# Scores for the maximum in four quarters through one PSUM bank of their own, and six PSUM banks for the layers after the last exp

## What is computed

```python
s = jnp.einsum('bqhd,bkhd->bhqk', q, k) * scale
s = jnp.where(mask, s, jnp.finfo(s.dtype).min)   # only in the first block
a = jax.nn.softmax(s, axis=-1)
return jnp.einsum('bhqk,bkhd->bqhd', a, v)
...
h = jax.nn.gelu(xm @ mlp_W1 + mlp_b1, approximate=True)
h = jax.nn.silu(jnp.einsum('btc,ecr->bter', combined, e_w1) + e_b1)
g = jax.nn.sigmoid(jax.nn.silu(combined @ gate_w1 + gate_b1) @ gate_w2 + gate_b2)
```

## Time and profile before

| | |
|---|---|
| median of 3 runs | 800.41 us (796.43 to 803.18) |
| profiled execution | 800.15 us, span 798.3 us |
| PE busy | 648.6 us (81%) |
| PE weight loads busy | 364.3 us (46%) |
| DVE busy | 431.4 us (54%) |
| ACT busy | 419.8 us (53%) |
| POOL busy | 220.0 us (28%) |
| mean granted TensorE clock | 0.944 |

### The profile page before, as it was taken

The page is one execution under the profiler, slowest core; times in us unless marked ns, Lnnn a source line. Parts: engine busy times, 40 slices in busy tenths (PEclk is TensorE's granted clock), DMA queues, the critical chain, the costliest instruction groups (busy, mean ns, idle before and its releaser), DMA issues.

```text
span 798.3 us, 16559 instructions
## 1 busy us (share of the span) xinstructions
PE 648.6 (81%) x6694; PEld 364.3 (46%) x6732; DVE 431.4 (54%) x1121; ACT 419.8 (53%) x714; POOL 220.0 (28%) x319
## 2 busy tenths in 40 slices
PE   5579887888879987888788878888899788868887
PEld 5234443444444544445345444543456443644445
DVE  2447767646665676566655666666555652231222
ACT  0141634555465464736474457365676639465453
POOL 3142433305341434323431334143131420000000
PEclk9689999998989999999999899999999989989899
DMA  8500000000000000000000000000000000000000
GB/s 302 175 2 1 16 1 15 14 2 28 15 1 2 15 14 15 2 14 15 16 1 2 24 5 2 15 1 15 1 2 14 2 1 2 0 14 1 0 14 13
DMA packets 15314, 15.81 MB, mean 20 GB/s; under 512 B 1833, under 2 KB 13108, under 8 KB 14856
## 3 DMA queue, kind: packets, MB, share of 16 engines
q1 hardware_dynamic: 14572, 10.72, 4.5%
q10 hardware_dynamic: 668, 4.05, 1.3%
HBM read 13.66 MB, written 1.09 MB: 18 GB/s over the span
## 4 chain that ended last, share of the span: by engine, by line
PE 51%; ACT 27%; DVE 15%; issue 4%; POOL 1%; DMA 1%; SPq 0%; DVEq 0%; ACTq 0%; POOLq 0%
ACT P L576 13%; PE lin L938 12%; PE lin L951 9%; PE big L1027 8%; PE avp L1055 6%; DVE mhl L773 5%; PE big L1006 3%; ACT hT L559 3%; ACT xn L548 2%; PE big L1034 2%; DVE bst L725 2%; PE big L1022 2%; ACT hid L610 2%; PE lin L960 2%; DVE oT L805 1%
## 5 line engine op out<-in xcount | busy, mean ns | idle before, releaser
L773 DVE TENSOR_REDUCE mhl<-big 128x8 bf16<-128x616 f32 (+1 forms) x160 | 151.0, 963 | 95.0 <-PE big L1006 92.6
L504 POOL TENSOR_TENSOR qm<-qT,hm 128x512 f32<-128x512 f32 x80 | 88.0, 1100 | 125.8 <-ACT qT L541 77.3
L938 PE MATMUL lin<-hT,W 128*128 128x512 f32 x184 | 107.7, 673 | 14.5 <-ACT hid L610 6.1
L576 ACT ACTIVATE P<-big,padcol 128x1024 f32<-128x1024 f32 x64 | 67.9, 1114 | 73.0 <-PE big L1034 73.0
L576 ACT ACTIVATE P<-big 128x1024 f32<-128x1024 f32 x64 | 62.0, 1021 | 78.0 <-PE big L1034 77.9
L1027 PE MATMUL big<-qm,kT 32*128 32x512 f32 x640 | 99.7, 695 | 0.0
L467 POOL TENSOR_SCALAR rstd<-mv 128x4 f32<-128x4 f32 (+1 forms) x36 | 8.4, 233 | 313.7 <-DVE mv L731 313.5
L1055 PE MATMUL avp<-P,Vp 128*32 128x128 f32 x2560 | 91.0, 285 | 1.3 <-DVE Vp L740 1.2
L490 POOL TENSOR_TENSOR kbm<-kT,hm 128x308 bf16<-128x308 f32 (+1 forms) x80 | 68.2, 853 | 58.0 <-PE big L1006 47.9
L1055 PEld LDWEIGHTS avp<-P,Vp 128*32 128x32 f32 x2560 | 68.2, 113 | 29.0 <-issue 24.5
L1006 PE MATMUL big<-kbm,qb 32*128 32x308 bf16 (+1 forms) x320 | 54.6, 342 | 29.0 <-ACT P L576 27.5
(11 more groups left out here) (160 smaller groups left out, 929.7 us busy)
## 6 DMA issues: line engine op xcount, KB each, us to landing
gring<-gate_rows SPq DMA_DIRECT2D x20, 256.0 KB, 3.5
W<-in_w ACTq DMA_DIRECT2D x2, 1152.0 KB, 12.3
hid<-in_ws SPq DMA_DIRECT2D x2, 832.0 KB, 5.5
W<-in_w ACTq DMA_DIRECT2D x1, 1088.0 KB, 7.3
x<-in_x SPq DMA_DIRECT2D x4, 256.0 KB, 9.9
out<-x SPq DMA_DIRECT2D x4, 256.0 KB, 2.0
ctx<-in_ctx SPq DMA_DIRECT2D x4, 154.0 KB
ctxT<-in_ctxT SPq DMA_DIRECT2D x4, 154.0 KB
```

Of the source, the lines that this page charges most:

```text
L504: nc.gpsimd.tensor_tensor(qm[:, j % 2], q.broadcast_to([128, 4, T]), mask.broadcast_to([128, 4, T]), ALU.mult).then_inc(qm_ready, 1)
L576: nc.scalar.activation(P[:, 8 * half:8 * half + 8, :], big[:, 2 * half:2 * half + 2, :].rearrange("p g (h q) -> p (g h) q", h=4), ACT.Exp, ...
L773: v.tensor_reduce(mhl[:].rearrange("p (g c) -> p g c", c=32)[:, 2 * half:2 * half + 2, 0:4], big[:, 2 * half:2 * half + 2, 0:4 * kw].rearr ...
L938: i = mm(lin_ap(st, s, job, m)[:, 0:n], w, a, start=(c == 0), stop=(c == len(parts) - 1))
```

## The change

- The scores for the maximum get a bank of their own, `sc`, of one bank (`GQ` = 1). They come in four quarters (`NQ` = 4) of one group of heads, and a quarter of job u + 1 stands in each slot of job u. A quarter is written when the maximum of the quarter before it has been read from `sc` (a wait for `m_ready`).
- `big` holds only transposed scores. `scores_t(u)` waits for both exps of job u - 1 (`st_free`), and the subtraction is a function of its own, `subtract(u)`, in slot 1. The exps move to slot 1 with it.
- `av(u - 1)` moves from slot 3 to the start of slot 0 of the next job, ahead of `turn(u)`.
- `normalise` is cut in two: two instructions in slot 0 behind the first quarter's maximum, two in slot 1 (`normalised`).
- `keep_warm` and its bank go; the transposed maxima go to a free part of the bank `avp`.
- Behind `END`, the layer units go round six banks (two of `lin`, four of `big`).
- The chains of layer units start two slots later and end two slots earlier.

```diff
@@
+NQ = 4
+GQ = 4 // NQ
+NLIN = 2
...
-TAILS = [(16 * 14, 16 * 18), (16 * 17, END + 16), (16 * 19, END + 60), (END + 16, END + 76)]
+TAILS = [(16 * 14 + 2, 16 * 18), (16 * 17 + 2, END + 16), (16 * 19 + 2, END + 60), (END + 16, END + 76)]
...
-    end = 16 * POS[k, s] - 6
+    end = 16 * POS[k, s] - 8
     if k:
-        return 16 * (POS[k - 1, s] + 1), end
+        return 16 * (POS[k - 1, s] + 1) + 2, end
...
+    if _kind == "END":
+        _ended, _next = True, 0
...
+            _bank = _next % (NLIN + 4 if _ended else NLIN)
+            _uses[_bank] += 1
+            LIN_AT[(_u[0], _s, _job)] = _bank, _uses[_bank]
...
-        mtpf = ps("mtp", [128, 512])
-        mtp = mtpf[:].bitcast(BF16)
+        sc = ps("sc", [128, GQ, 512])
+        mtp = avp[:].bitcast(BF16)[:, 4 * T:5 * T]
...
-                elif kind == "A" and s == 0:
+                elif kind == "A" and s == 1:
                     exps(u, 0)
                     exps(u, 1)
...
-            def maxima(j, half):
+            def maxima(j, part):
 
                 kw = ATT[job_of(j)[0]]["kw"]
-                dve.wait_ge(s_full, job_turn(j, half, 2))
+                dve.wait_ge(s_full, job_turn(j, part, NQ))
...
                     if s == 0:
                         turned(u)
-                        if u > 0:
-                            normalise(u - 1)
-                    elif s < 3 and u + 1 < JOBS:
-                        maxima(u + 1, s - 1)
+                    if u + 1 < JOBS and s % GQ == 0:
+                        maxima(u + 1, s // GQ)
+                    if u > 0 and s == 0:
+                        normalise(u - 1)
+                    if u > 0 and s == 1:
+                        normalised(u - 1)
...
-            def scores(j, half):
+            def scores(j, part):
...
-                pe.wait_ge(st_free, job_turn(j, half, 2))
-                for g in (2 * half, 2 * half + 1):
-                    o = big[:, g, 0:4 * kw].rearrange("p (h k) -> p h k", h=4)
+                if j + part > 0:
+                    pe.wait_ge(m_ready, NQ * j + part)
+                groups = range(GQ * part, GQ * part + GQ)
+                for g in groups:
+                    o = sc[:, g % GQ, 0:4 * kw].rearrange("p (h k) -> p h k", h=4)
...
-                pe.wait_ge(m_ready, job_turn(j, 1, 2))
+                pe.wait_ge(st_free, job_turn(j, 1, 2))
                 if a == 0:
...
+            def subtract(j):
+
                 pe.wait_ge(mt_ready, job_turn(j))
...
-            def keep_warm(n):
-
-                for _ in range(n):
-                    mm(mtpf[:], identb[:], oneb[:], start=True, stop=True)
...
                     if s == 0:
+                        if u > 0:
+                            av(u - 1)
                         turn(u)
+                    if u + 1 < JOBS and s % GQ == 0:
+                        scores(u + 1, s // GQ)
+                    if s == 0:
                         scores_t(u)
-                        if u in IDLE:
-                            keep_warm(3)
-                    elif s == 3:
-                        av(u)
-                    elif u + 1 < JOBS:
-                        scores(u + 1, s - 1)
+                    if s == 1:
+                        subtract(u)
+                elif kind == "END":
+                    av(JOBS - 1)
```

More of the change, by code:

```diff
@@ L172 @@
     UNITS += [("B", u, s) for slot, u, s in PLACED if slot == _slot]
-IDLE = [j for j in range(JOBS) if not any(slot == 4 * j and u[1] not in ("stat", "apply") for slot, u, s in PLACED)]
 UNITS += [("END", None, None)] + [("B", u, s) for slot, u, s in PLACED if slot >= END]
-LIN_AT, _n = {}, 0
+LIN_AT, _uses, _ended, _next = {}, [0] * (NLIN + 4), False, 0
 for _kind, _u, _s in UNITS:
+    if _kind == "END":
+        _ended, _next = True, 0
     if _kind == "B" and _u[1] not in ("stat", "apply"):
         for _job in ([_u[1] + "a", _u[1] + "b"] if _u in (("p0", "q"), ("p0", "k")) else [_u[1]]):
-            LIN_AT[(_u[0], _s, _job)] = _n
-            _n += 1
+            _bank = _next % (NLIN + 4 if _ended else NLIN)
+            _uses[_bank] += 1
+            LIN_AT[(_u[0], _s, _job)] = _bank, _uses[_bank]
+            _next += 1
 def lin_bank(st, s, job):
-    return LIN_AT[(st, s, job)] % 2
+    return LIN_AT[(st, s, job)][0]
 def lin_turn(st, s, job):
-    return LIN_AT[(st, s, job)] // 2 + 1
+    return LIN_AT[(st, s, job)][1]
 def order_of(s, *wanted):
@@ L349, in build @@
         bias_mm = sem("bias_mm")
-        lin_full = [sem(f"lin_full{i}") for i in range(2)]
-        lin_free = [sem(f"lin_free{i}") for i in range(2)]
+        lin_full = [sem(f"lin_full{i}") for i in range(NLIN + 4)]
+        lin_free = [sem(f"lin_free{i}") for i in range(NLIN + 4)]
         ln_bn, ln_stats, ln_eps, ln_pow, ln_rstd, ln_xn = ([sem(f"{n}{s}") for s in range(NS)] for n in (
@@ L389, in lin_ap @@
         def lin_ap(st, s, job, p=128):
-            return lin[0:p, lin_bank(st, s, job), :]
+            i = lin_bank(st, s, job)
+            return lin[0:p, i, :] if i < NLIN else big[0:p, i - NLIN, :]
         def diag(s, kw):
@@ L486, in keys @@
                 if j >= 2:
-                    pool.wait_ge(s_full, job_turn(j - 2, 1, 2))
+                    pool.wait_ge(s_full, job_turn(j - 2, NQ - 1, NQ))
                 k = kT[s][:, b * kw:(b + 1) * kw].unsqueeze(1)
@@ L651, in chain @@
                 dve.wait_ge(setup_dve, n_setup[0])
-            v.memset(rowb[:], 0.0).then_inc(lin_free[0], 1)
+            v.memset(rowb[:], 0.0)
+            for i, free in enumerate(lin_free):
+                v.memset(rden[:, i, :], 0.0).then_inc(free, 1)
             chain(v.memset(mcb[:], 0.0))
-            v.memset(rden[:], 0.0).then_inc(lin_free[1], 1)
             v.memset(oneb[:], 1.0)
@@ L767, in project @@
                     v.tensor_copy(qb[s][:], qT[s][:]).then_inc(qb_ready, 1)
-            def maxima(j, half):
+            def maxima(j, part):
                 kw = ATT[job_of(j)[0]]["kw"]
-                dve.wait_ge(s_full, job_turn(j, half, 2))
-                v.tensor_reduce(mhl[:].rearrange("p (g c) -> p g c", c=32)[:, 2 * half:2 * half + 2, 0:4],
-                                big[:, 2 * half:2 * half + 2, 0:4 * kw].rearrange("p g (h k) -> p g h k", h=4), AX,
+                dve.wait_ge(s_full, job_turn(j, part, NQ))
+                v.tensor_reduce(mhl[:].rearrange("p (g c) -> p g c", c=32)[:, GQ * part:GQ * part + GQ, 0:4],
+                                sc[:, :, 0:4 * kw].rearrange("p g (h k) -> p g h k", h=4), AX,
                                 ALU.max).then_inc(m_ready, 1)
@@ L874, in _ @@
                 if kind == "START":
-                    for half in range(2):
-                        maxima(0, half)
+                    for part in range(NQ):
+                        maxima(0, part)
                 elif kind == "A":
@@ L984, in project @@
                     tokens(st, s, "v", [kv], [W[:, VBLK[a], :]], t=A["kw"])
-            def scores(j, half):
+            def scores(j, part):
                 a, s, b = job_of(j)
                 kw = ATT[a]["kw"]
-                if half == 0:
+                if part == 0:
                     if b == 0:
@@ L1009, in turn @@
             def turn(j):
-                pe.wait_ge(m_ready, job_turn(j, 1, 2))
-                nc.tensor.transpose(mtp[:, 0:T], mhl[:], identb[:]).then_inc(mt_full, 1)
+                pe.wait_ge(m_ready, job_turn(j, NQ - 1, NQ))
+                nc.tensor.transpose(mtp, mhl[:], identb[:]).then_inc(mt_full, 1)
             def scores_t(j):
@@ L1149, in _ @@
                     pe.wait_ge(rows_in, 48)
-                    for half in range(2):
-                        scores(0, half)
+                    for part in range(NQ):
+                        scores(0, part)
                 elif kind == "A":
                     if s == 0:
+                        if u > 0:
+                            av(u - 1)
                         turn(u)
+                    if u + 1 < JOBS and s % GQ == 0:
+                        scores(u + 1, s // GQ)
+                    if s == 0:
                         scores_t(u)
-                        if u in IDLE:
-                            keep_warm(3)
-                    elif s == 3:
-                        av(u)
-                    elif u + 1 < JOBS:
-                        scores(u + 1, s - 1)
+                    if s == 1:
+                        subtract(u)
+                elif kind == "END":
+                    av(JOBS - 1)
                 elif kind == "B":
```

10 lines of the change are left out of this document (6 added, 4 removed).

## The result

The changed kernel takes 899.21 us (898.31 to 901.32), the kernel before 801.79 (796.43 to 807.0) in the same comparison: 1.122 times as long, 95% interval 1.114 to 1.130. The forecast was 792.5, the range 768 to 820. It was wrong in sign and far outside its range.

What follows compares the result with a forecast made beforehand. PE was taken to set the pace; loop terms −17 + 32 − 20 + 5 − 2 = −2 us and −6 us at the ends made −8 us on 800.15, stated as 792.5 us, range 768 to 820.

Steps and rivals of the forecast that it cites:

- part 3: Loop: maxima ahead of the layer work, quarters 2 and 3 under the exps; waits for DVE fall, −20 us.
- part 6: Start and tail: start +2.4 us, six tail banks −7.0, fewer matmuls behind the last exps −1.7; sum −6 us.
- part 1: Loop: score waits for exps and keep_warm go, a 57 us hole under the exps comes; net −17 us.
- Rival (a): Loop: one score bank makes PE and DVE walk in step; +34 us, 826 us, chance 0.15.
- Part 5: Granted clock in the loop: some slow stretches go, new ones may come without keep_warm; net −2 us.
- rival (b): Loop: without keep_warm PE falls to 1.2 GHz in 15 to 20 stretches; +25 us, 818 us, chance 0.10.
- Part 2: Loop: score matmuls in quarters instead of halves run one by one on PE; +32 us (26 to 54).
- Part 4: ACT in the loop: eight more table loads, about half hidden, and layer units ahead of exps; +5 us.

Runs made afterwards that it cites:

- experiment 1: Changed kernel with one layer bank and two score banks: 935.8 us, against 991.7 us with one layer bank and one score bank.
- experiment 4: Kernel before with keep_warm alone taken out: 827.88 us, 1.039 times the kernel before.
- experiment 7: Kernel before in its old order, without keep_warm, with score quarters through one bank, each waiting for the maximum before it: 1041.2 us, 1.303 times.
- experiment 6: Kernel before with scores and maxima in four quarters, but through the four banks of big, so no quarter waits for a maximum: 813.26 us, 1.019 times.
- the control of experiment 1: Changed kernel with one layer bank instead of two, one score bank as before: 991.7 us, one run.

## Why the prediction was wrong

- **The step that failed: part 3, "quarters 2 and 3 lie under the exps", with the wait for the maximum put at nothing.** The exps take 1.94 to 2.12 us. Behind the subtraction PE and DVE go round the ring twice (matmul, maximum, two semaphores), 1.5 and 1.8 us in the masked job above, with 1.29 us of `normalise` in it. My own numbers would have shown it for these jobs: part 6 has a masked quarter at 0.64 + 0.68 + 0.1 = 1.42 us, and two of them are 2.84. In job 45, with 77 keys, the exps do cover the ring. But part 1 had PE's layer matmuls fill the time under the exps and part 3 had the ring wait there as well; a quarter that waits at the head of PE's queue holds those matmuls up. The waits for DVE at the scores came to 95.7 us, all of them ahead of quarters 2 and 3; some 60 us of them delay P times V by the estimate above, and with one layer bank a second score bank is worth about 56 us (experiment 1). Quarters 0 and 1 were covered, as I had said.
- **Rival (a) was the mechanism and was priced at a third.** I had 34 us, 24 of them in the 24 residual units, and its sign (waits of over 25 us) came. Its price missed that DVE's work for the jobs themselves holds the ring too. Of the 98.6 us of these waits in the whole span, DVE had a layer instruction between the quarter and its maximum for 52.6, `normalise` or the copy of the maxima for 33.1, and neither for 13.0. Its "longer than what PE has left under the exps" holds: where PE has layer matmuls there, the waits come on top.
- **Part 1.** The waits for the exps went (42.6 to 3.0), as forecast; the hole of 57 us under the exps never appeared, because the quarters and layer matmuls that stand ahead of P times V filled it and more.
- **Part 5, rival (b).** I set the clock at −2 us net and gave its fall as 25 us. `keep_warm` alone is 29 us in the kernel before (experiment 4), and the clock goes from 0.95 to 0.88 in the loop, under the 0.92 that I had named as the sign. Its return gives only 9 to 13 us in the changed kernel. The two causes were treated as rivals with separate prices. They came together: with the same 6618 matmuls and a ring, the clock fell further, from 0.902 to 0.812 (experiments 4 and 7).
- **Part 2.** Its masked jobs were priced at 11.2 + 6.1 = 17.3 us; experiment 6, which tests these and the added reductions, gave 15. The 15.0 us of the 48 jobs without a mask stay untested.
- **Part 3, the gain.** The transpose of the maxima and the subtraction waited 21.1 + 8.3 = 29.4 us for DVE. In the changed kernel the transpose waits 14.1 and the subtraction not at all: 15 us went, where I had 20.
- **Part 4.** The table loads are 57 instead of 49 and ACT is busy for 9.5 us more, as I had it; what this costs in time no run shows.
- **Part 6.** Right in size: the tail is 7.8 us shorter (forecast 8.7), the six banks are worth 11 to 14 us in the two kernels (forecast 7, at most 14). The start cost 4.7 where I had 2.4.
- **The sum.** My terms add up to −8 us, 792.1 from 800.15, not 792.5. Nothing hangs on it.

The account, as far as it is measured, in the kernel before: +29 (`keep_warm`) +15 (quarters) −11 (tail) = +33 of 98. These prices need not add: in the changed kernel `keep_warm` is worth 9 to 13 us, not 29. The other 65 us or more hold the ring with its slow clock, the single score matmuls and the table loads, less what the new order gives back. How they split stays open: each experiment on the ring moved the clock too (shorter maxima 0.908). The slots can't be priced apart from the order.

## What to carry to other kernels

- A buffer that one engine fills and another drains makes a ring of both. Count its round trip, semaphores and the reader's other work included, times the turns in a job, and set it beside the time that is said to cover it. If the filling engine has other work under the same cover, add that. The reader's share of busy time (51% here) is no argument.
- A bank given to one stage is taken from another: here a layer bank was worth about 92 us, a second score bank about 56. The banks that a stage leaves for good are free, and using them was the only one of the parts tried alone in the kernel before that made it faster.
- Before idle filler work is removed, remove it alone in the old kernel and read the granted clock.

## What the runs showed of the hardware

- Matmuls whose result nobody reads, 25 us of them in the trace, are worth 29 us: without them the mean granted clock is 0.902 instead of 0.944, and the other matmuls are busy for 30 us longer. The Trainium skill, "TensorE: Matmul & The Clock Gate", What's actually happening, has the slow level as the default that activity releases; these runs agree.
- A DVE tensor_tensor of 128x128 float32 in SBUF takes 0.27 to 0.29 us with no GpSimd instruction beside it (20 of the 80 in the changed kernel). Where GpSimd's `qm` was already running (44 of them) it took 0.80 us on average, up to 1.10. The mean of all 80 is 576 ns against 363 when the instruction is moved away.
- The waits of TensorE come with a lower clock. With 6618 matmuls in both, the ring of experiment 7 had 0.812 to 0.824 in four runs and experiment 4, without a ring, 0.893 to 0.915. One layer bank less went with 0.862 instead of 0.886 (the control of experiment 1, one run).
